# Gated slot attention, 4 x 512 tokens: keys times queries with tokens in partitions, inverse sums turned for it, value weights and heads one projection later, single stores

## The reference

```python
q, k, v, s = heads(n @ Wq), heads(n @ Wk), heads(n @ Wv), clip(heads(n @ Ws), -32, 32)
z = cumlogsumexp(s, axis=time)
g = exp(z_before - z);  p = exp(s - z)
# step_k:  hk = hk * g_t + k_t p_t^T ;  ok_t = q_t hk       (key memory, 64 x 64)
pv = softmax(ok)                                           # over the 64 slots
# step_v:  hv = hv * g_t + p_t v_t^T ;  o_t = pv_t hv       (value memory, 64 x 128)
o = o * rsqrt(mean(o^2) + eps) * g_norm_weight * silu(n @ Wg)
x = x + o @ Wo
x = x + down(silu(gate(n2)) * up(n2))                      # fp8-rounded weights
```

## Time and profile before

| | before |
|---|---|
| median of 3 runs | 1384.22 us (1383.70 to 1384.83) |
| profiled execution: its own time | 1384.27 us |
| profiled execution: span from first to last instruction | 1382.6 us |
| PE busy | 1357.9 us, 98% of the span |
| PE weight loads | 1118.4 us, 81% |
| DVE busy | 1046.3 us, 76% |
| ACT, POOL busy | 401.0 us, 138.4 us |
| granted TensorE clock | 0.999 of full speed |
| DMA | 114 MB, the 16 engines a third busy |

### The profile page before, as it was taken

How to read it: one execution, slowest core, us unless ns; L and a number is a source line. 1 busy time by engine, 2 the same in 40 slices (tenths; PEclk the granted TensorE clock), 3 DMA queues, 4 the chain that set the end, 5 groups by cost and what they waited for, 6 DMA issues and landing times.

```text
span 1382.6 us, 21680 instructions
## 1 busy us (share of the span) xinstructions
PE 1357.9 (98%) x8047; PEld 1118.4 (81%) x8047; DVE 1046.3 (76%) x1650; ACT 401.0 (29%) x1181; POOL 138.4 (10%) x106
## 2 busy tenths in 40 slices
PE   6999999999999999999999999999999999999998
PEld 5788888888888888888888888888888878888886
DVE  8878878887888788778877887888778775535354
ACT  4322323332332233223322332233222323222221
POOL 3001101110110012001200110011010010000000
PEclk9999999999999999999999999999999999999999
DMA  6143334433533353335334433443121440000000
GB/s 183 45 124 92 86 84 123 98 87 82 129 90 83 82 130 87 87 84 136 89 84 96 114 86 86 106 113 81 41 81 28 134 122 1 31 1 30 0 31 31
DMA packets 307668, 113.99 MB, mean 82 GB/s; under 512 B 240496, under 2 KB 291312, under 8 KB 307568
## 3 DMA queue, kind: packets, MB, share of 16 engines
q1 hardware_dynamic: 307568, 112.67, 32.8%
HBM read 70.60 MB, written 42.01 MB: 81 GB/s over the span
## 4 chain that ended last, share of the span: by engine, by line
PE 93%; DVE 5%; issue 1%; DMA 1%; SPq 0%; POOL 0%; ACT 0%; DVEq 0%
PE bank L444 19%; PE bank L446 18%; PE bank L445 18%; PE bank L117 13%; PE bank L1563 6%; PE bank L650 4%; PE bank L580 4%; PE bank L633 3%; PE bank L505 2%; PE bank L567 2%; DVE wvg_lo L977 2%; PE bank L638 2%; PE bank L598 1%; PE bank L611 1%; PE bank L620 1%
## 5 line engine op out<-in xcount | busy, mean ns | idle before, releaser
L444 PE MATMUL bank<-wvg_hi,xT_hi 128*128 128x512 f32 x512 | 208.8, 408 | 0.0
L446 PE MATMUL bank<-wvg_hi,xT_lo 128*128 128x512 f32 x512 | 200.3, 391 | 0.0
L445 PE MATMUL bank<-wvg_lo,xT_hi 128*128 128x512 f32 x512 | 199.8, 390 | 0.0
L711 ACT ACTIVATE a_and_v<-bank 128x256 f32<-128x256 f32 x128 | 49.0, 382 | 286.3 <-PE bank L446 286.3
L1112 DVE TENSOR_TENSOR y<-y,bank 128x512 f32<-128x512 f32 x128 | 86.9, 684 | 49.4 <-PE bank L446 49.3
L444 PEld LDWEIGHTS bank<-wvg_hi,xT_hi 128*128 128x128 f32 x512 | 96.3, 188 | 21.5 <-issue 0.8
L446 PEld LDWEIGHTS bank<-wvg_hi,xT_lo 128*128 128x128 f32 x512 | 96.1, 188 | 21.0
L445 PEld LDWEIGHTS bank<-wvg_lo,xT_hi 128*128 128x128 f32 x512 | 96.5, 188 | 17.3
L997 DVE RECIPROCAL cT<-cT 128x512 f32<-128x512 f32 x32 | 107.3, 3354 | 1.1
L444 PE MATMUL bank<-wo_hi,oT_hi 128*128 128x512 f32 x256 | 105.9, 414 | 0.0
L949 POOL TENSOR_TENSOR rstd<-ssq,neg_half 128x8 f32<-128x8 f32 x32 | 52.3, 1636 | 491.1 <-DVE ssq L1049 491.1
(11 more groups left out here) (162 smaller groups left out, 3040.4 us busy)
## 6 DMA issues: line engine op xcount, KB each, us to landing
o_transposed<-o SPq DMA_DIRECT2D x108, 128.0 KB, 2.7
oT_lo<-o_transposed SPq DMA_DIRECT2D x108, 128.0 KB, 2.7
fp_weights<-q SPq DMA_DIRECT2D x28, 318.0 KB, 2.6
e_tokens<-k_tok_then_wT SPq DMA_DIRECT2D x124, 64.0 KB, 2.2
e_tok<-e_tokens SPq DMA_DIRECT2D x124, 64.0 KB, 2.0
k_tokens<-p SPq DMA_DIRECT2D x124, 48.0 KB, 2.1
k_tok_then_wT<-k_tokens SPq DMA_DIRECT2D x124, 48.0 KB, 1.9
...
```

The lines of the kernel that those rows point to most:

```text
L444: pe.matmul(dst, w_hi, m_hi, start=(k == 0), stop=False)
L445: pe.matmul(dst, w_hi, m_lo, start=False, stop=False)
L446: last = pe.matmul(dst, w_lo, m_hi, start=False, stop=(k == n - 1))
```

## The change

1. **Scores with tokens in partitions.** The product that gave `ok` with slots in partitions, both heads and 256 moving columns in one matmul (8 matmuls, line 580 of before), becomes 16 matmuls that take the masked scores as weights, 64 columns at a time, and move 64 columns of e; 6 matmuls of 128 moving columns make the value states. The state part swaps its operands in the same way. `ok` lies in T0, the value states in T1.
2. **One set of transposes.** The transposes into T0 (line 611) go: maximum, subtraction, exponential, sum and the second scaling by 1/C run on `p` with tokens in partitions; then one set turns `p` into T1, and ACT instead of DVE copies it to `wT`.
3. **Inverse sums.** 1/C has to lie with tokens in partitions too. DVE turns its blocks in each unit (in `sums`), SP stores it and loads it (`store_c`, `load_c`) like e and k. `c_sum` and `c_tok` are the two former buffers `cT`. The first unit transposes it on PE.
4. **Order.** The output product runs in one piece; `VG1` moves ahead of the value weights and `VG2` ahead of the masked product. On DVE `out_norm` goes behind `key_states` and `o_turn` behind `value_states`; before, both stood ahead of `clip`. `e_turn` and `add_y` go behind the softmax's steps, `sums` ahead of `mask_value_weights`. The key states' sums go into bank A[0] instead of O[0] up to unit 27.
5. **Stores.** Each store through DRAM is one DMA with runs of 128 floats instead of four with runs of 32; the four loads now gather runs of 32 floats, where they read whole rows before.

```diff
-    ok_of = [pair_bank[:, c // 2, (c % 2) * P:(c % 2 + 1) * P] for c in range(CH)]
-    hv_of = [pair_bank[:, c // 2, (2 + c % 2) * P:(3 + c % 2) * P] for c in range(CH - 1)]
-    ok_both = pair_bank[:, :, 0:2 * P]
+    c_sum, c_tok = cT[0][:, :], cT[1][:, :]
+    ok_of = [T0[:, c * P:(c + 1) * P] for c in range(CH)]
+    hv_of = [T1[:, c * P:(c + 1) * P] for c in range(CH - 1)]
 
...
+    def hk_bank(u):
+
+        return A[0] if u <= FAR + 1 else O[0]
...
 
+        def store_blocks(dram, tile, signal):
+
+            sp.dma_start(dram.rearrange("c p f -> p c f"), tile.rearrange("p (c f) -> p c f", f=P)).then_inc(signal, 16)
+
+        def load_blocks(tile, dram, signal):
+
+            n = dram.shape[0] * BL
+            for b in range(BL):
+                sp.dma_start(tile[BK * b:BK * (b + 1), :].rearrange("t (n m) -> t n m", n=n),
+                             dram.rearrange("c (i t) f -> t (c i) f", t=BK)[:, :, BK * b:BK * (b + 1)]
+                             ).then_inc(signal, 16)
...
+        def store_c(nu):
+
+            sp.wait_ge(s_cb, nu)
+            store_blocks(c_dram, c_sum, s_cst)
+
+        def load_c(nu):
+
+            sp.wait_ge(s_cst, 16 * nu)
+            sp.wait_ge(s_wm, nu)
+            load_blocks(c_tok, c_dram, s_cld)
...
-                pe.wait_ge(s_sub, u)
-                pe.wait_ge(s_wT, u)
+                pe.wait_ge(s_oks, u)
...
+        def w_transposes(u):
+
+            pe.wait_ge(s_wm, u + 1)
+            for c in range(CH):
+                mm = pe.transpose(T1[:, c * P:(c + 1) * P], p[:, c * P:(c + 1) * P], ident[:, :])
+            mm.then_inc(s_trw, 1)
...
-                pe.wait_ge(s_oev, 2 * u)
+                if u > FAR + 1:
+                    pe.wait_ge(s_oev, 2 * u)
+                else:
+                    pe.wait_ge(s_bm, 2 * u)
...
             for c in range(CH):
                 for a in range(2):
+                    at = slice(M * a, M * (a + 1))
+                    for h in range(2):
+                        ts = slice(64 * h, 64 * (h + 1))
+                        pe.matmul(ok_of[c][ts, at], av[par][:, a, c, 0, ts], e_tok[:, c, at],
+                                  start=(c == 0 and a == 0), stop=(c == 0), skip_group_check=True)
+            for c in range(CH - 1):
+                for a in range(2):
                     hs, at = slice(64 * a, 64 * (a + 1)), slice(M * a, M * (a + 1))
-                    both = 2 if c < CH - 1 else 1
-                    dst = pair_bank[hs, c // 2, :].rearrange("p (n s t) -> p n s t", n=2, s=2)[:, 0:both, c % 2, :]
-                    mm = pe.matmul(dst, e_tok[:, c, at], av[par][:, a, c, 0:both, :],
-                                   start=(c % 2 == 0), stop=(c == 0), skip_group_check=True)
+                    mm = pe.matmul(hv_of[c][hs, :], e_tok[:, c, at], av[par][:, a, c, 1, :],
+                                   start=(c == 0), stop=(c == 0), skip_group_check=True)
             mm.then_inc(s_hvd, 1)
...
+            if first:
+                pe.wait_ge(s_cinv, 1)
+                for c in range(CH):
+                    mm = pe.transpose(A[1][:, c * P:(c + 1) * P], c_sum[:, c * P:(c + 1) * P], ident[:, :])
+                mm.then_inc(s_trc, 1)
             pe.wait_ge(s_hk, 2 * (u + 1))
-            pe.wait_ge(s_hv, 3 * (u + 1))
             for c in range(1, CH):
-                mm = pe.matmul(ok_of[c], hk[:, c - 1, :], qT[:, c * P:(c + 1) * P],
+                mm = pe.matmul(ok_of[c], qT[:, c * P:(c + 1) * P], hk[:, c - 1, :],
                                start=False, stop=True, skip_group_check=True)
             mm.then_inc(s_ok, 1)
+            if not first:
+                pe.wait_ge(s_oev, 2 * u)
             v = product_of(u)
-            if v is not None:
+            if v is None:
+                job(QT, nu, ni)
+            else:
                 pe.wait_ge(s_oh, 2 * (v + 1))
                 pe.wait_ge(s_ol, 2 * (v + 1))
                 if v % B == 0:
                     pe.wait_ge(s_wl, 5 * (v // B) + 5)
-                out_product(v, (0, 1))
-
-            pe.wait_ge(s_oks, u + 1)
-            for c in range(CH):
-                mm = pe.transpose(T0[:, c * P:(c + 1) * P], p[:, c * P:(c + 1) * P], ident[:, :])
-            mm.then_inc(s_trs, 1)
-            if v is not None:
-                out_product(v, (2, 3))
-            if not last:
+                out_product(v, range(CH))
+            pe.wait_ge(s_hv, 3 * (u + 1))
+            w_transposes(u)
+            if v is not None and not last:
                 job(QT, nu, ni)
-
-            pe.wait_ge(s_exp, u + 1)
-            for c in range(CH):
-                mm = pe.transpose(T1[:, c * P:(c + 1) * P], p[:, c * P:(c + 1) * P], ident[:, :])
-            mm.then_inc(s_trw, 1)
             if not last:
                 job(VG0, nu, ni)
+                job(VG1, nu, ni)
             else:
                 ffn.gate_product(pe, 0, 1, early=True)
 
...
             if not last:
                 scores(nu)
-                job(VG1, nu, ni)
+                job(VG2, nu, ni)
...
-            job(VG2, nu, ni)
             job(VG3, nu, ni)
...
+        def wT_evac(u):
+
+            act.wait_ge(s_trw, u + 1)
+            if u + 1 < UNITS:
+                act.wait_ge(s_est, 16 * (u + 1))
+            copy(wT[:, :], T1[:, :]).then_inc(s_wT, 1)
...
             act.activation(p[:, :], p[:, :], ACT.Exp).then_inc(s_exp, 1)
+            if product_of(u) is not None:
+                wT_evac(u)
             if last:
                 ffn.fuse_hi(act, 0, 0)
                 ffn.tanh(act, 0, 1)
             if not last:
                 evac(QT, nu, ni)
+            if product_of(u) is None:
+                wT_evac(u)
...
             dve.wait_ge(s_e, u + 1)
-            dve.tensor_tensor_scan(cT[i % 2][:, :], eT[i % 2][:, :], eT[i % 2][:, :], 0.0, ALU.add,
+            if u == 1:
+                dve.wait_ge(s_trc, 1)
+            elif u:
+                dve.wait_ge(s_cst, 16 * (u - 1))
+            dve.tensor_tensor_scan(c_sum, eT[i % 2][:, :], eT[i % 2][:, :], 0.0, ALU.add,
                                    ALU.bypass).then_inc(s_scan, 1)
             dve.wait_ge(s_scan, u + 1)
-            dve.reciprocal(cT[i % 2][:, :], cT[i % 2][:, :]).then_inc(s_cinv, 1)
+            dve.reciprocal(c_sum, c_sum).then_inc(s_cinv, 1)
+            if u:
+                dve.wait_ge(s_cinv, u + 1)
+                dve.transpose(c_sum, c_sum).then_inc(s_cb, 1)
...
-            if not first:
-                out_norm(u - 1)
-            if u and u - 1 <= FAR:
-                o_turn(u - 1)
+            if not last:
+                clip(nu, ni)
             if u == FAR + 2:
                 for c in range(CH):
                     add_y(FAR, c)
-            if not last:
-                clip(nu, ni)
             key_states(u)
+            if not first:
+                out_norm(u - 1)
             value_states(u)
+            if u and u - 1 <= FAR:
+                o_turn(u - 1)
             if u > FAR + 1:
                 out_lo(u - 1, A)
...
-            if not last:
-                e_turn(nu, ni)
...
             dve.wait_ge(s_ok, u + 1)
-            dve.wait_ge(s_cinv, u + 1)
-            if not first:
-                dve.wait_ge(s_trw, u)
-                dve.wait_ge(s_kst, 16 * BL * u)
-            dve.scalar_tensor_tensor(out=p[:, :].rearrange("p (n t) -> p n t", n=2), in0=ok_both, scalar=SCALE,
-                                     in1=cT[i % 2][:, :].rearrange("p (n t) -> p n t", n=2),
+            if first:
+                dve.wait_ge(s_ctok, 1)
+            else:
+                dve.wait_ge(s_cld, 16 * BL * u)
+                dve.wait_ge(s_kst, 16 * u)
+            dve.scalar_tensor_tensor(out=p[:, :], in0=T0[:, :], scalar=SCALE, in1=c_tok,
                                      op0=ALU.mult, op1=ALU.mult).then_inc(s_oks, 1)
+            dve.wait_ge(s_oks, u + 1)
+            dve.tensor_reduce(mx[:, :], p3, AX.X, ALU.max).then_inc(s_max, 1)
+            dve.wait_ge(s_max, u + 1)
+            dve.tensor_tensor(p3, p3, mx[:, :].rearrange("p (s a) -> p s a", a=1).broadcast_to([P, 2 * CH, M]),
+                              ALU.subtract).then_inc(s_sub, 1)
             v = product_of(u)
             if last:
                 ffn.times_gate(dve, 0, 0)
-                add_y(v, 0)
+            else:
+                e_turn(nu, ni)
+            dve.wait_ge(s_exp, u + 1)
+            dve.tensor_reduce(sm[:, :], p3, AX.X, ALU.add).then_inc(s_sum, 1)
+            dve.wait_ge(s_sum, u + 1)
+            dve.tensor_tensor(p[:, :], p[:, :], c_tok, ALU.mult).then_inc(s_wm, 1)
+            dve.scalar_tensor_tensor(out=es[:, :], in0=sm[:, :], scalar=EPS, in1=sm[:, :],
+                                     op0=ALU.mult, op1=ALU.mult).then_inc(s_es, 1)
+            if last:
                 ffn.times_up(dve, 0, 0)
-            elif v is not None:
+            if v is not None:
                 add_y(v, 0)
                 add_y(v, 1)
-
```

(47 more changed lines are left out.)

95 lines of the change are left out of this document (36 added, 59 removed).

## The result

The changed kernel takes 1406.41 us (median of 4 runs, 1405.27 to 1406.74), the kernel before beside it 1384.32: ratio 1.0158, 95% interval 1.0146 to 1.0171. It is 1.6% slower. In the profiled executions the span went from 1382.6 to 1404.6 us, 22.0 more, and that is what has to be found.

The account below looks back on a forecast made before the run. Bound by PE's own work plus 0.60 us in each of seven units. Terms -0.2 + 6.2 + 6.4 + 0.9 - 0.7 = +12.6 on 1384.27 us gave 1396.9, 0.9% slower; range 1385 to 1409.

Parts of the forecast that it names:

- The forecast case: Whole kernel: DVE's later chain and collisions with GpSimd outweigh PE's savings, +12.6 us, 1389 to 1404; chance 0.63.
- rival 3: Sixteen small matmul pairs on PE don't run side by side, +0.94 us a unit; 1407 us in all; chance 0.12.
- What PE saves: On PE, per unit: four transposes of line 611, 0.35 us, and one start of a group, 0.16; together 0.51.
- The plain stall: Units with i = 1 or 4: PE waits 0.46 us for far_lo before the output product; -0.02 a unit.
- the moved projections only trade places: On PE: moving VG1 and VG2 leaves the number of groups otherwise the same; no cost was given for it.
- i = 2: Seven units: GpSimd's ws_lo runs on top of DVE's out_norm, delaying the chain 0.9 us; +0.88 each, +6.2 in all.
- i = 3: Seven units: far_lo on DVE collides with GpSimd's work, PE stalls 1.99 us; +0.91 each, +6.4 in all.
- Units 0 and 1: No output product hides the softmax there: +0.6 us in unit 0, +0.3 in unit 1, +0.9 together.
- The tail: Four last units: PE's transposes of o wait for out_norm's second half; -0.48 + 0.3 each, -0.7 us in all.
- The softmax: Plain units: p ready at S + 10.4 us, wanted at S + 11.8, no wait; S starts PE's key-state sums.
- Rivals 1 and 2: DVE is in time everywhere, 1371 us, chance 0.06; and GpSimd costs nothing new, 1380 us, chance 0.09.
- rival 1: DVE is in time everywhere because its steps overlap more: -13.5 us, so 1371; chance 0.06.

Follow-up runs that it names:

- e1: The changed kernel with DVE's old order put back, out_norm and o_turn ahead of clip again: 1384.53 us, ratio to before 0.9999.
- e9: The changed kernel with the edits of e1 and e4, and in units with i = 2 far_hi and far_lo at the unit's start: 1370.8 us.
- e4: The changed kernel with ACT's split of the second half of Wo behind the evacuation of VG1, not ahead of it: 1403.9 us.
- e3: The changed kernel, but in units with i = 2 GpSimd starts its low part of the new weights only after far_lo: 1398.02 us.
- e5: The kernel before with only DVE's new order: clip first, out_norm behind key_states, o_turn behind value_states: 1425.88 us.
- e7: e4 with the stores and loads of e and k in the form of the kernel before: 1403.96 us.

## Why the prediction was right, and where its terms were not

The sign, the place and the main mechanism held: PE's work shrinks and the chain through `far_lo` on DVE takes it back; e1 shows that the order on DVE costs as much as the change lost. The forecast case gave +12.6 us and the kernel took +22. Its 1406.4 us lie above the forecast's own ends, 1389 to 1404; the range up to 1409 holds them only by the part that was added for rival 3, whose mechanism the trace refutes. That much is luck. Term by term:

- **What PE saves.** Forecast 0.51 less 0.03 for the small matmuls, 0.48; shown 0.40, in every unit with i = 4 of e1 and e9. Of the 0.08, 0.06 lie ahead of the output product: in the unit with i = 4 of e9 PE reaches it at S + 5.85, before at S + 5.76, 0.09 later where I took 0.03, nearly all of it in the products of the scores and value states (591.01 - 589.32 = 1.69 against 1.62). From there to `VG0` the unit is 0.35 shorter, the transposes as forecast. The remaining projections save 0.14, where one start less was to be worth 0.16. The 32 matmuls of 64 columns in pairs take 590.25 - 589.32 = 0.93 us, 0.91 ns a column. Rival 3, by whose mechanism they would have taken nearly twice that, gave 1407 and so the measured time, but is refuted: right number, wrong cause. The floor of about 62 ns for each such instruction, which the Trainium skill, "TensorE: Matmul & The Clock Gate", section on the 56 ns gap, gives for decoding in software, is not seen here: 32 in 0.93 us, two side by side, is 29 ns each.
- **The plain stall.** Forecast 0.46, measured 0.58. `far_lo` starts at S + 5.04, not 4.92: the copy of `hv` starts 0.03 after `out_norm`'s end (591.63), where I let it overlap by 0.09. `oT_lo` ends at S + 6.29 and PE goes on 0.15 later, at S + 6.44, where I had allowed 0.05 and 6.25 in all; PE would have come at S + 5.86 instead of 5.79. The matmuls behind the wait then run 0.04 closer, so the unit loses 0.54: it is at +0.14 and not -0.02. For the 12 plain units that is 1.9 us.
- **i = 1.** Forecast as plain. Three of six lost another 0.5 to 1.2, all six together 2.7 us, which e4 gave back (2.5). This step failed: "the moved projections only trade places". They don't: with `VG1` the second gate went ahead of the masking of the value weights on DVE, that gate needs the tanh on ACT, and ACT's queue, which the change left as it was there, has 36.2 us of waits for Wo ahead of it. The prediction never went through that queue. The list of the changes in order doesn't name the gate's move either; the diff shows it.
- **i = 2.** The mechanism held, the size did not: +1.39, forecast +0.88. The collision costs 1.11, where I took 0.9 between 0.69 and 1.30. The other 0.28 is the plain 0.14 and as much again. Of that, 0.11 lie between the end of `oT_lo` and PE's first output matmul: in the changed kernel and in e3 this takes 0.26 us or a little more with i = 2, and 0.15 in every other unit. In these units PE's queue has one more wait there, for the low part of new Wo weights; that it is the cause is not shown (in e5 the lag with i = 2 is 0.10). By the rule of the Trainium skill, "SBUF — State Buffer", section on the two sides, that one of the two engines blocks the other for a whole instruction, it would have been 1.30; the trace agrees with it nearly, since `ws_lo` lasted 1.48 from 520.95 and `out_norm`'s first half had the port before.
- **i = 3.** Held: +0.98, forecast +0.91. `oT_lo` ended at 561.38, S + 7.72, as forecast (549.2 - 541.47 = 7.73).
- **Units 0 and 1** cost +1.5, forecast +0.9; PE's wait for `p` is there, 3.4 us in two. **The tail**: -0.7 in units 28 to 30, forecast -0.7 for four; unit 31 is not in the table. **The softmax**: `p` is ready at 599.06, S + 10.45, forecast S + 10.4, and PE asks later. **The transfers** of e and k cost nothing by their form, as e7 shows.

Together the terms miss 9.1 us: 3.5 in i = 2, 3.6 in i = 1, 1.0 in i = 4, 0.5 in i = 3, 0.6 in the first two. Rivals 1 and 2 are refuted for the changed kernel; rival 1's number, 1371, is what the kernel gives once DVE is in time (e9, 1370.8). Its sum comes out by errors that cancel: it leaves out the 0.60 that seven units with i = 3 would win back (4.2 us), and counts 0.08 too much in each unit and 0.6 too little in units 0 and 1.
